# A third transposed-batch buffer, a later grid count and four parts of inverse deviations in a graph-network kernel on one core

## What is computed

```python
h = relu(layernorm(x))
degv = A.sum(0) + A.sum(1) - diagonal(A)
Ln   = D^-1/2 (diag(degv) - A) D^-1/2
_, U = eigh(Ln)                                   # 120 x 120, once
agg = einsum('vn,bvd->bnd', U, h)
o   = relu(agg @ W1 + b1) @ W2 + b2
# theta, phi, g: products over the nodes; phi and g max-pooled by 2
y   = softmax(theta^T phi) @ g                    # 1024 x 512 per batch
z   = batchnorm(wo @ y) + o
out = x + einsum('nv,bvd->bnd', U, z) + z
```

## Time and profile before

| what | us |
|---|---|
| median of three runs | 3327.8 |
| the three runs | 3327.76, 3327.80, 3329.16 |
| the profiled execution, its own time | 3326.99 |
| its span, first to last instruction | 3325.2 |
| PE busy in the span | 3168.9 (95%) |
| DVE busy | 2322.8 (70%) |
| ACT busy | 2411.2 (73%) |
| POOL busy | 1890.5 (57%) |
| mean granted TensorE clock | 0.993 of full |

### The profile page before, as it was taken

How to read it: one execution, slowest core, us unless ns; L and a number is a source line. 1 busy time by engine, 2 the same in 40 slices (tenths; PEclk the granted TensorE clock), 3 DMA queues, 4 the chain that set the end, 5 groups by cost and what they waited for, 6 DMA issues and landing times.

```text
span 3325.2 us, 65809 instructions
## 1 busy us (share of the span) xinstructions
PE 3168.9 (95%) x16040; PEld 2546.6 (77%) x16040; DVE 2322.8 (70%) x6363; ACT 2411.2 (73%) x4380; POOL 1890.5 (57%) x1718
## 2 busy tenths in 40 slices
PE   6888987799999999999999999999999999999997
PEld 4677776577777777777777777777777777777775
DVE  7998888766666666666666666666666666666664
ACT  6889999666666666666666666666666666666665
POOL 3222211166666666666666666666666666666665
PEclk9999999899999999999999999999999999999998
DMA  3334443212222222222222222222222222222222
GB/s 100 93 100 108 111 114 104 66 50 72 73 73 73 73 73 73 74 72 72 72 72 72 72 72 72 72 72 72 72 72 72 72 72 73 74 72 72 73 72 66
DMA packets 111574, 256.21 MB, mean 77 GB/s; under 512 B 47500, under 2 KB 49797, under 8 KB 111493
## 3 DMA queue, kind: packets, MB, share of 16 engines
q1 hardware_dynamic: 111493, 255.25, 28.2%
HBM read 190.69 MB, written 63.44 MB: 76 GB/s over the span
## 4 chain that ended last, share of the span: by engine, by line
PE 80%; DVE 16%; issue 3%; POOL 1%; DMA 0%; ACT 0%; DVEq 0%; POOLq 0%; ACTq 0%
PE ps_M L802 8%; PE ps_M L803 8%; PE ps_M L804 8%; PE ps_S L879 7%; PE ps_E L802 7%; PE ps_O L802 7%; PE ps_E L803 7%; PE ps_O L804 7%; PE ps_E L804 7%; PE ps_O L803 7%; PE ps_M L863 3%; DVE ST L1133 1%; DVE row L1019 1%; DVE rown L1033 1%; DVE zt L1023 1%
## 5 line engine op out<-in xcount | busy, mean ns | idle before, releaser
L505 POOL TENSOR_TENSOR p_lo<-p,p_hi 128x512 fp32r<-128x512 f32 x1024 | 1383.5, 1351 | 929.4 <-ACT p_hi L656 928.3
L651 ACT ACTIVATE p<-ps_E 128x512 f32<-128x512 f32 x1024 | 613.6, 599 | 332.4 <-PE ps_E L804 307.4
L1410 DVE TENSOR_REDUCE nmx<-ps_S 128x1 f32<-128x512 f32 x1024 | 658.6, 685 | 125.2 <-PE ps_S L879 123.9
L656 ACT ACTIVATE p_hi<-p 128x512 fp32r<-128x512 f32 x1024 | 647.2, 632 | 32.6
L802 PE MATMUL ps_E<-o_hi,Q_hi 123*128 123x512 f32 x1024 | 426.9, 417 | 0.0
L802 PE MATMUL ps_O<-p_hi,v_hi 128*121 128x512 f32 x1024 | 407.3, 398 | 4.2 <-POOL p_lo L505 4.2
L804 PE MATMUL ps_O<-p_lo,v_hi 128*121 128x512 f32 x1024 | 406.7, 397 | 0.0
L804 PE MATMUL ps_E<-o_lo,Q_hi 123*128 123x512 f32 x1024 | 404.2, 395 | 0.0
L803 PE MATMUL ps_E<-o_hi,Q_lo 123*128 123x512 f32 x1024 | 404.2, 395 | 0.0
L803 PE MATMUL ps_O<-p_hi,v_lo 128*121 128x512 f32 x1024 | 404.1, 395 | 0.0
L1390 DVE TENSOR_REDUCE gf<-ps_M 128x256 f32<-128x512 f32 x256 | 177.1, 692 | 262.6 <-PE ps_M L804 262.6
(11 more groups left out here) (364 smaller groups left out, 5947.3 us busy)
## 6 DMA issues: line engine op xcount, KB each, us to landing
rbc<-r_dram SPq DMA_DIRECT2D x128, 484.0 KB
xin<-in_x_dram SPq DMA_DIRECT2D x128, 480.0 KB, 4.2
xt<-in_x_dram SPq DMA_DIRECT2D x128, 480.0 KB, 5.0
out_dram<-y SPq DMA_DIRECT2D x128, 480.0 KB, 3.7
o_hi<-mrow SPq DMA_DIRECT2D x256, 2.0 KB
dcol<-y SPq DMA_DIRECT2D x128, 4.0 KB, 2.0
r_dram<-rcol SPq DMA_DIRECT2D x128, 4.0 KB, 1.4
W1s<-in_L_gnn_W_dram SPq DMA_DIRECT2D x1, 512.0 KB, 4.3
```

Of the source, the lines that this page charges most:

```text
L505: pool.tensor_tensor(p_lo[:, c % 4, :], p[:, c % 4, :], p_hi[:, c % 4, :].bitcast(F32), ALU.subtract).then_inc(plo_sb, 1)
L651: act.activation(p[:, c % 4, :], ps_E[c % 2][:, :], ACT.Exp).then_inc(p_sb, 1)
L656: act.activation(p_hi[:, c % 4, :], p[:, c % 4, :], ACT.Copy).then_inc(phi_sb, 1)
L1410: dve.tensor_reduce(nmx[:, c:c + 1], ps_S[SBANK[c]][:, :], AX.X, ALU.max, negate=True).then_inc(max_sb, 1)
```

## The change

1. `junkx` is no tile of its own: the scratch results go into the part of `P1` that the last four batches fill, and the copy of batch B-4 waits until all squares are done.
2. `fT` has three buffers; its copies of batch s wait for the product of batch s-3.
3. All of ScalarE's slots are written out, where slots 4 to 93 were a loop.
4. In the last slot the squares come behind the `fT` copies.
5. `rstds` is done in four parts (64, 32, 16 and 16 batches), three of them ahead of the two one-column powers, and the clearing of `xt` comes ahead of those powers.
6. `GRID_AT` is 102 where it was 99.

```diff
-            junkx = eb("junkx", [N, D], BF16)
-            fT = eb("fT", [128, 2, KC * N])
+            junkx = P1[0:N, (B - 4) * H:B * H].bitcast(BF16)
+            fT = eb("fT", [128, 3, KC * N])
...
             rstds(0, B // 2)
+            rstds(B // 2, B * 3 // 4)
+            rstds(B * 3 // 4, B * 7 // 8)
+            pool.wait_ge(wy_ps, WY_P(7) + 1)
+            pool.memset(xt[0:1, :, :], 0.0).then_inc(xt_free, 1)
             pool.wait_ge(dve_out, 5)
             pool.tensor_tensor(pv[:, 6:7], pv[:, 5:6], colA[:, 10:11], ALU.pow).then_inc(pool_out, 1)
...
-            pool.wait_ge(wy_ps, WY_P(7) + 1)
-            pool.memset(xt[0:1, :, :], 0.0).then_inc(xt_free, 1)
-            rstds(B // 2, B)
-            pool.wait_ge(rstd_done, 2)
+            rstds(B * 7 // 8, B)
+            pool.wait_ge(rstd_done, 4)
...
-                late(act, w1_done, s - 1)
+                late(act, w1_done, s - 2)
                 for j in range(2):
-                    last = act.activation(fT[:, par, j * 4 * N:(j + 1) * 4 * N], ps_T[par][:, j, 0:4 * N], ACT.Copy)
+                    last = act.activation(fT[:, s % 3, j * 4 * N:(j + 1) * 4 * N], ps_T[par][:, j, 0:4 * N], ACT.Copy)
...
+                if s == B - 4:
+                    act.wait_ge(sq_done, B)
...
-                if not fixed or k < B:
+            def slot(k):
+                par = k % 2
+                if k < B:
                     b_relu(k, par)
+                if k < B - 1:
                     b_sq(k, par)
-                if not fixed or 0 <= k - 2 < B:
+                if 0 <= k - 2 < B:
                     b_ft(k - 2, par)
+                if k == B - 1:
+                    b_sq(k, par)
...
-            for k in range(4):
-                slot(k, k % 2)
-            rounds(act, 4, WY_SLOT, slot)
-            for k in range(WY_SLOT, B + 4):
-                slot(k, k % 2)
+            for k in range(B + 4):
+                slot(k)
...
-                last = mm(ps_m[par][0:N, 0:H], fT[:, par, c * N:(c + 1) * N], W1s[:, c, :],
+                last = mm(ps_m[par][0:N, 0:H], fT[:, s % 3, c * N:(c + 1) * N], W1s[:, c, :],
...
-GRID_AT = 99
+GRID_AT = 102
```

More of the change, by code:

```diff
@@ L527, in b_sum @@
             def b_sum(s, par):
-                act.wait_ge(x_in[par], s * 8 + 16 - 8 * par)
-                act.activation(junkx[:, :], xin[:, par, :], ACT.Copy, scale=-1.0 / D,
+                act.wait_ge(x_in[par], (s // 2 + 1) * 16)
+                act.activation(junkx, xin[:, par, :], ACT.Copy, scale=-1.0 / D,
                                accum_out=lns[:, par, 0:1]).then_inc(mean_done, 1)
@@ L538, in b_sq @@
                 act.wait_ge(mean_done, s + 1)
-                act.activation(junkx[:, :], xin[:, par, :], ACT.Square, bias=lns[:, par, 0:1],
-                               accum_out=rstd[0:N, bass.ds(s, 1)]).then_inc(sq_done, 1)
+                act.activation(junkx, xin[:, par, :], ACT.Square, bias=lns[:, par, 0:1],
+                               accum_out=rstd[0:N, s:s + 1]).then_inc(sq_done, 1)
             def b_ft(s, par):
                 act.wait_ge(tr_done, s + 1)
-                late(act, w1_done, s - 1)
+                late(act, w1_done, s - 2)
                 for j in range(2):
-                    last = act.activation(fT[:, par, j * 4 * N:(j + 1) * 4 * N], ps_T[par][:, j, 0:4 * N], ACT.Copy)
+                    last = act.activation(fT[:, s % 3, j * 4 * N:(j + 1) * 4 * N], ps_T[par][:, j, 0:4 * N], ACT.Copy)
                 last.then_inc(ft_done, 1)
@@ L550, in b_p1 @@
                 act.wait_ge(w1_done, s + 1)
-                act.activation(P1[0:N, bass.ds(s * H, H)], ps_m[par][0:N, 0:H], ACT.Copy).then_inc(p1_done, 1)
-            def slot(k, par):
-                fixed = isinstance(k, int)
-                if not fixed or k < B:
+                if s == B - 4:
+                    act.wait_ge(sq_done, B)
+                act.activation(P1[0:N, s * H:(s + 1) * H], ps_m[par][0:N, 0:H], ACT.Copy).then_inc(p1_done, 1)
+            def slot(k):
+                par = k % 2
+                if k < B:
                     b_relu(k, par)
+                if k < B - 1:
                     b_sq(k, par)
-                if not fixed or 0 <= k - 2 < B:
+                if 0 <= k - 2 < B:
                     b_ft(k - 2, par)
-                if not fixed or k + 1 < B:
+                if k == B - 1:
+                    b_sq(k, par)
+                if k + 1 < B:
                     act.wait_ge(sq_done, k + 1)
                     b_sum(k + 1, 1 - par)
-                if not fixed or 0 <= k - 4 < B:
+                if 0 <= k - 4 < B:
                     b_p1(k - 4, par)
@@ L598, in factor @@
                     keep((QA[:, N:2 * N], ps_V[0:N, 128:128 + N], 1.0))
-            for k in range(4):
-                slot(k, k % 2)
-            rounds(act, 4, WY_SLOT, slot)
-            for k in range(WY_SLOT, B + 4):
-                slot(k, k % 2)
-                if k < WY_SLOT + WY_STEPS:
+            for k in range(B + 4):
+                slot(k)
+                if WY_SLOT <= k < WY_SLOT + WY_STEPS:
                     factor(k - WY_SLOT)
```

## The result

| what | before | changed |
|---|---|---|
| median of 18 runs each, us | 3328.45 | 3334.77 |
| lowest to highest | 3325.90 to 3329.89 | 3334.07 to 3337.07 |
| the profiled execution, us | 3326.99 | 3334.53 |
| its span | 3325.2 | 3332.8 |

The medians are 6.3 us apart. The ratio on record is 1.0021, with a 95% interval of 1.0015 to 1.0027 (5 to 9 us): slower, and right at the 0.2% that the prediction took as what a measurement can tell from no change. 3337.3 was forecast, between 3332 and 3341.

The account below looks back on a forecast made before the run. VectorE's eigenvector chain was taken to bound the preparation stage. The profiled 3327.0 us plus 8.0 (count) and 1.5 (tail) gave 3336.5; with the median 0.8 above it, 3337.3 us was forecast, range 3332 to 3341.

Parts of the forecast that it names:

- The bound: Preparation stage: VectorE's eigenvector chain sets its end; ScalarE's gains help only where VectorE or TensorE waits for it.
- The count: Grid count, three batches later: starts at 510.0 us, releasing VectorE and bringing Z 8.0 us later, between 6.6 and 9.0.
- ScalarE's lead: How much earlier ScalarE is by the grid count: 0.95 us from written-out loop and third buffer, ends 0 and 2.4.
- the buffer's 0.5: Third fT buffer's part of ScalarE's lead at the grid count: 0.5 us, at most 1.95.
- The tail: Z to setup_done: TensorE idles some 16 us before Z, then half clock slows its products; 1.5 us, between 0 and 1.9.
- The main stage's start: After setup_done: already at half clock before, so 0, with ends of -4 and +2 us.
- second rival: Main stage begins at full clock and the tail costs little: 3333.3 us, within 0.2% of before; chance 0.12.
- The other edits at nothing: Preparation stage: scratch into P1, last squares, rstds in parts, earlier clearing of xt, each priced at 0.
- first rival: The lead carries TensorE to the grid count in time: not slower, deciding from a 3.7 us lead on; chance 0.06.
- half of the clock's ends: Range's allowance for the clock at the main stage's start: 2.4 us off the low end, 2 on the high.
- the powers hold VectorE: Rival: GpSimd's 32- and 16-column powers add 5.3 + 2.6 us to VectorE's sweep by the shared port: 3345.2 us; chance 0.03.

Follow-up runs that it names:

- g99: The changed kernel with GRID_AT back at 99, all else as changed; 3327.54 us, 0.9998 of before.
- b102: The kernel before with GRID_AT = 102 alone; 3336.34 us, 1.0024 of before.
- warm102b: The changed kernel with 67 extra identity products, results unused, on TensorE ahead of Z's transposition; 3333.45 us, 1.0017 of before.
- halves102: The changed kernel with the inverse deviations in two parts again (64 and 64 columns); 3332.62 us, 1.0018 of before.
- g100tail: The changed kernel with GRID_AT = 100 and the vectors' products behind the products of batches 126 and 127; 3326.71 us, 0.9994 of before.
- warmA: g100tail with 18 extra identity products ahead of Z's transposition and 13 behind the last weight product; 3323.41 us, 0.9988 of before.
- g100: The changed kernel with GRID_AT = 100, all else as changed; 3329.08 us, 1.0003 of before.
- tail102: The changed kernel, GRID_AT still 102, with the vectors' products behind the products of batches 126 and 127; 3334.53 us, 1.0020 of before.
- two_ft: The changed kernel with two fT buffers again and the wait for the product of batch s-2; 3336.65 us, 1.0024 of before.
- warm102: The changed kernel with 60 extra identity products, results unused, on TensorE ahead of Z's transposition; 3334.41 us, 1.0019 of before.
- poolsplit: g100tail with the splitting of W2 and the theta weights moved from VectorE to GpSimd, during the eigenvalue sweeps; 3330.02 us, 1.0006 of before.
- warmB: g100tail with only the 13 extra identity products behind the last weight product; 3324.15 us, 0.9991 of before.

## Why the prediction was right, and where its sizes were off

**The bound.** Right. VectorE's chain ends the stage; ScalarE's losses at the count are free (g99), a wait of VectorE there is not (b102).

**The count.** Right in its place: forecast 510.0, measured 510.02. That it agrees to 0.02 us is luck: `MJ` to the count spreads by 0.66 us between equal kernels, and the sum took 0.45 us from the weights' transposition to the count, where it is 0.22 in the changed kernel. VectorE was released 7.76 us later, not 8.0, since I had compared starts of the count. The count itself had run at half clock before (0.59 us from its start to VectorE's copy) and ran at full clock now (0.31). Then `Z` came 7.38 us later: VectorE got back 0.38 on the way, in two steps of about 0.2 beside the places where GpSimd's 64-column powers had begun before. The runs do not isolate that. ScalarE's lead was put at 0.95 and is 0.91 in the pair of changed and b102; given the same spread, that agreement is partly luck too, and the buffer's 0.5 in it came from a working whose rows are not shown.

**The tail.** Forecast +1.5 with 1.9 as the full price; measured +1.76. The named cause is shown by warm102b. The two products were priced 1.07 and 0.3 on the path; the first alone cost 1.67 (3.59 against 1.92), as the half clock held all through it where at the count it had returned on the way, and the second cost nothing, as the clock came back at 642.0.

**The main stage's start.** I took 0 between -4 and +2; it was -1.59 in the profiled pair, less than the 3.8 us by which kernels with the same tail differ. 1.26 of it lie ahead of the first score product: the clock was at full until 648.85, 1.6 us into the stage, and again for 3.4 us from 652.26, where before it had been at half from 639.35 to 653.00. That is what the second rival described, seen beside the forecast in this one execution; that the change brings it about is not shown.

**The other edits at nothing.** Right within what the times tell: g99 is at 0.9998, halves102 no different from the changed kernel. The clearing of `xt` was priced only by when `xt` is needed; beside VectorE's sweep it can cost some 0.5 us (g99), and in the changed kernel it happened not to. The name's "vectors' products behind the last batch's" was indeed not done by the change; done in g100tail it takes 2.55 us from the tail.

**The sum.** Forecast 9.5 us, measured 6.3. Of the 3.2 us, 0.6 are VectorE's release and what it got back, 1.6 the main stage, and -0.3 the tail. The remaining 1.2 us are no part of the mechanism: the two profiled executions differ by 7.5 us and the medians by 6.3, because the one of before lay 1.5 us under its later median and the changed one 0.2 under its own. The forecast took the same offset of 0.8 for both. So the agreement within the range rests on the two terms of the count and the tail, and the measured 3334.77 is nearer to the second rival's 3333.3 than to 3337.3. The range did not follow its own rule, half of the clock's ends: 2.4 and 2 were taken where the halves of -4 and +2 are 2 and 1, which would give 3332.4 to 3339.7 and holds the result as well. And the first rival's lead would have to be 3.75 us, not 3.7, to bring the sum under 6.7.

**The rivals.** That the lead carries TensorE to the count in time is refuted by the 8.25 us of VectorE's stand. That the powers hold VectorE is refuted, as VectorE's time from the count's copy to `Z` was 127.69 us after and 128.07 before; but another GpSimd operation moved by the same edit, the clearing of `xt`, did hold it in g99.

**Open.** Why the start of `MJ` moves by up to 3.6 us between executions. And what decides the clock at which the main stage starts, and how much of the differences of 1 to 4 us in the main stage it makes: in the first 60 us behind `setup_done` half clock was granted for 10.2 us in warmA, halves102 and g100, 17.1 in the kernel before, the changed kernel, b102 and warm102b, and 20.5 to 21.3 in g100tail, tail102, two_ft and warm102. From `setup_done` to the end the three groups took 2683.5 to 2686.6, 2685.1 to 2687.1 and 2686.3 to 2688.7 us. They rise together, but overlap, and a single execution of each can't settle the size or the cause.

## What to carry to other kernels

Where two engines' chains meet at one place of a fixed list, a stand of the chain with slack is free and a stand of the chain that ends last is paid in full: place the meeting where the chain that ends last arrives, and let the other one wait. When one engine's work is finished earlier than the path needs it, look at what the pause does to TensorE's clock in the few products that are still on the path, and move work that nobody waits for out from between those that somebody does. A gain of 2 us at one point is not won until the times show it, and a single trace of the next stage can't say why they don't: look first at how far traces of kernels with the same start of that stage lie apart. Before work is moved to an idle engine or to another place of its list, look at what runs beside it there.

## What the runs showed of the hardware

GpSimd operations differ in what they do to VectorE. Beside the power on 64 columns (10.6 us) VectorE ran on as usual. Beside a subtraction of 128 by 1024 elements from two SBUF inputs, one VectorE operation with two SBUF inputs took exactly the 2.37 us of GpSimd's, and beside the cast another took its 1.04. The rule of the Trainium skill (SBUF — State Buffer, Who interferes with whom), by which GpSimd holds the port that it shares with VectorE for its whole operation and shuts out operations with two SBUF inputs, thus agrees with these two and not with the power; I had taken as evidence against the rule, and it is evidence about the power alone. A clearing, which reads nothing, let operations with two SBUF inputs run at 0.20 us beside it, but a TENSOR_SCALAR on 120 by 2 elements that took 0.16 us in g100 lasted until the clearing's end, 0.76 us in g99 and 1.30 in poolsplit, and so did the operation behind it.

TensorE's clock can be lost by a short pause, and what it costs falls on the work behind the pause. In warm102, with products up to 2 us ahead of the transposition, it fell 0.8 us after that transposition had started; with 67 products and a pause of 0.50 us it stayed up through the tail and was lost 0.9 us after `setup_done`. 31 products without use, 7 us of TensorE's time that nobody wanted, went with a time 3.7 us under that of before. Against g100tail, which lacks only them, the ratios are 0.9988 and 0.9994, some 2 us apart with intervals that overlap, so a gain by them is not shown. In warmB half clock was granted for 3.4 us from 619.3 in the midst of batch work, where TensorE's longest pause in the 13 us before was 1.1 us. Nor does the clock at the main stage's start follow from the edits alone: with and without such products (warmA and halves102) it was granted at the same mean, 0.78 of full, in the 23 us behind `setup_done`.
